# Ternary feed-forward: row transposes by DMA instead of by TensorE, and two roundings moved to ScalarE

## The reference, cut to what matters

```
def _quant_weight(w):                      # ternary
    scale = jnp.mean(jnp.abs(w)) + EPS
    return jnp.clip(jnp.round(w / scale), -1.0, 1.0) * scale
def _quant_act(x):                         # 8 bits, one scale for each row
    scale = jnp.maximum(jnp.max(jnp.abs(x), axis=-1, keepdims=True), EPS) / 127.0
    return jnp.clip(jnp.round(x / scale), -128.0, 127.0) * scale
def bitlinear(x, w): return einsum('bsi,oi->bso', _quant_act(x), _quant_weight(w))

gate = sigmoid(bitlinear(layernorm(x), w_gate))     # 512 -> 2048
up   = bitlinear(layernorm(x), w_up)                # 512 -> 2048
x    = x + tanh(g_ffn[0]) * bitlinear(gate * up, w_down)    # 2048 -> 512
```

## Time and profile before

| | us |
|---|---|
| median of 3 runs | 1298.64 (1296.31 to 1298.73) |
| the profiled execution | 1298.14 |
| its span, first to last instruction | 1296.4 |
| the feed-forward, 573 to 789 us of the span | about 216 |

### The profile page before, as it was taken

How to read it: one execution, slowest core, us unless ns; L and a number is a source line. 1 busy time by engine, 2 the same in 40 slices (tenths; PEclk the granted TensorE clock), 3 DMA queues, 4 the chain that set the end, 5 groups by cost and what they waited for, 6 DMA issues and landing times. The chain is left out here.

```text
span 1296.4 us, 14519 instructions
## 1 busy us (share of the span) xinstructions
PE 1108.1 (85%) x4802; PEld 449.3 (35%) x4802; DVE 1020.2 (79%) x1560; ACT 668.9 (52%) x783; POOL 526.6 (41%) x403
## 2 busy tenths in 40 slices
PE   4976399999999999838999994999999998189686
PEld 2543022222222222103444442444444444034232
DVE  5678498888888888218999982888888877777888
ACT  1645048787887887925566563110000000686896
POOL 5757010534534534530011012878887884000021
PEclk9989569999999999969999997999999998599879
DMA  9799633545445544132111101121221220000011
GB/s 321 244 317 339 197 107 118 158 125 169 139 126 170 139 125 153 53 126 83 49 49 32 49 17 36 49 60 55 65 65 49 65 65 16 0 1 1 0 66 65
DMA packets 65215, 131.74 MB, mean 102 GB/s; under 512 B 13864, under 2 KB 31656, under 8 KB 61552
## 3 DMA queue, kind: packets, MB, share of 16 engines
q1 hardware_dynamic: 65152, 130.95, 31.6%
HBM read 106.53 MB, written 22.02 MB: 99 GB/s over the span
## 5 line engine op out<-in xcount | busy, mean ns | idle before, releaser
L804 DVE TENSOR_REDUCE mneg<-ps_m 128x1 f32<-128x512 f32 x512 | 319.6, 681 | 53.0 <-PE ps_m L717 52.6
L1345 PE MATMUL ps_y<-kv,toeplitz_sb 128*128 128x512 f32 x640 | 279.4, 595 | 8.9 <-POOL kv L1257 8.9
L685 ACT ACTIVATE probs<-ps_s 128x1024 f32<-128x1024 f32 x256 | 250.9, 1022 | 51.8 <-PE ps_s L739 51.7
L717 PE MATMUL ps_m<-k_stack,q_stack 112*128 112x512 bf16 x512 | 186.6, 405 | 17.1 <-DMA k_stack<-mask_k 16.0
L1345 PEld LDWEIGHTS ps_y<-kv,toeplitz_sb 128*128 128x128 f32 x640 | 121.0, 191 | 155.2 <-issue 155.2
L739 PE MATMUL ps_s<-q_stack,k_stack 112*128 112x512 bf16 x512 | 153.3, 383 | 10.7 <-ACT probs L685 10.5
L749 PE MATMUL ps_o<-probs,v_all 128*17 128x512 f32 x1024 | 134.7, 598 | 0.4 <-ACT probs L685 0.4
L1257 POOL TENSOR_TENSOR kv<-vT,ctxT_sb 128x2048 f32<-128x2048 f32 x32 | 118.8, 3712 | 39.1 <-PE ps_y L1345 32.3
L980 PE MATMUL ps_g<-w,xT_f 128*128 128x512 bf16 x512 | 120.0, 383 | 7.1 <-DVE h_f L1127 6.3
L1411 DVE TENSOR_TENSOR z<-ps_y,ctxT_sb 128x1024 f32<-128x1024 f32 x64 | 77.9, 1217 | 47.1 <-PE ps_y L1345 47.1
L1310 ACT ACTIVATE w_anchor<-w_f 128x512 f32<-128x512 f32 x32 | 20.1, 628 | 180.6 <-DMA w_f<-in_w 180.6
(11 more groups left out here) (159 smaller groups left out, 1628.3 us busy)
## 6 DMA issues: line engine op xcount, KB each, us to landing
w_sweep<-in_w SPq DMA_DIRECT2D x8, 1536.0 KB, 10.2
q_stack<-q_parts SPq DMA_DIRECT2D x96, 128.0 KB, 4.1
k_stack<-k_parts SPq DMA_DIRECT2D x96, 128.0 KB, 3.9
w_sweep<-in_w SPq DMA_DIRECT2D x16, 768.0 KB, 5.5
w_sweep<-in_w SPq DMA_DIRECT2D x16, 512.0 KB, 3.5
toeplitz_sb<-in_toeplitz SPq DMA_DIRECT2D x32, 256.0 KB, 2.7
w_f<-in_w SPq DMA_DIRECT2D x32, 256.0 KB, 2.9
k_parts<-qk_part SPq DMA_DIRECT2D x24, 256.0 KB, 7.0
```

The costliest lines, as they stand in the source:

```text
L685: nc.scalar.activation(pr[:, k % 2, 2 * slot:2 * slot + 2, :], S[:, 2 * slot:2 * slot + 2, :], ACT.Exp).then_inc(exp_done, 1)
L717: nc.tensor.matmul(M[:, bank(j), :], Q[0:ROWS, slot, hd, tc * P:(tc + 1) * P], K[0:ROWS, slot, hd, :], start=True, stop=True).then_inc(max ...
L804: nc.vector.tensor_reduce(mneg[:, h, tile % LT, tile // LT:tile // LT + 1], M[:, bank(j), :], AX.X, ALU.max, negate=True).then_inc(max_red, 1)
L1345: mm = nc.tensor.matmul(Y[:, q % 3, l2, :], T[:, g % 2, (lt - m) * P:(lt - m + 1) * P], kv[:, g % 2, m, :], start=(m == 0), stop=(m == lt))
```

## The change

- Both transposes are DMAs on SP's queue: xT from xq and hT from hq, each one instruction (L932, L939). TensorE's transposes, the PSUM tiles XTP and HTP and ScalarE's copies `copy_x` and `copy_h` are gone.
- ScalarE centres the rows (`centre(t+2)`, behind the sigmoid of chunk 3) and rounds them (`round_x(t+1)`, two instructions, behind the sigmoid of chunk 1). VectorE's `prepare` keeps the maximum and the scales.
- `round_h(t-1)` moves from behind the sigmoid of chunk 1 to behind that of chunk 2, `take_down(t-2)` from behind that of chunk 2 to behind that of chunk 3 and `centre`.
- The maxima of h are two of 1024 columns (`half_max`) in place of four of 512. The maximum of the weight piece moves from chunk 2 to chunk 1.
- The four loads of ctxT (1 MB each) are issued in tile 0 behind the transposes of x, no longer ahead of everything.
- The loop over pairs of tiles is written out.

```diff
-    tile(0, 0, True, False)
-    tile(1, 1, False, False)
-    with eng.Fori(1, n // 2 - 1) as i:
-        tile(2 * i, 0, False, False)
-        tile(2 * i + 1, 1, False, False)
-    tile(n - 2, 0, False, False)
-    tile(n - 1, 1, False, True)
+    for t in range(n):
+        tile(t, t % 2, t == 0, t == n - 1)
...
+                def turn_x(t, par):
+                    sp.wait_ge(xq_ready, t + 1)
+                    if t >= 2:
+                        sp.wait_ge(gu_done, NCH * (t - 1))
+                    sp.dma_start(xT[:, par], xq[:, par, :], transpose=True).then_inc(xT_ready[par], 16)
+                def turn_h(t, par):
+                    sp.wait_ge(hq_ready, t + 1)
+                    if t >= 2:
+                        sp.wait_ge(down_done, t - 1)
+                    sp.dma_start(hT[:, par], hq[:, par, :], transpose=True).then_inc(hT_ready[par], 16)
...
+                    if not last:
+                        turn_x(t + 1, 1 - par)
+                    if not first:
+                        turn_h(t - 1, 1 - par)
+                    if first:
+                        for lt in range(LT):
+                            sp.dma_start(core.cT[:, lt], A["ctxT"][lt * P:(lt + 1) * P]).then_inc(core.cT_loaded, 16)
+                    if last:
+                        turn_h(t, par)
+                turn_x(0, 0)
                 over_tiles(sp, ROWT, tile)
...
-                def turn_x(t, par):
-                    pe.wait_ge(xq_ready, t + 1)
-                    for lt in range(LT):
-                        mm = nc.tensor.transpose(XTP[:, lt * P:(lt + 1) * P], xq[:, par, lt * P:(lt + 1) * P],
-                                                 core.ident16[:])
-                    mm.then_inc(xt_done, 1)
...
                         pe.wait_ge(d_taken, t)
-                    for half in range(2):
-                        pe.wait_ge(hT_ready, 2 * t + half + 1)
-                        for k in range(half * KT // 2, (half + 1) * KT // 2):
-                            mm = nc.tensor.matmul(D[:], hT[:, par, k, :], wd[:, k, :], start=(k == 0),
-                                                  stop=(k == KT - 1))
+                    pe.wait_ge(hT_ready[par], 16 * (t // 2 + 1))
+                    for k in range(KT):
+                        mm = nc.tensor.matmul(D[:], hT[:, par, k, :], wd[:, k, :], start=(k == 0), stop=(k == KT - 1))
                     mm.then_inc(down_done, 1)
...
-                        if c == 2 and not last:
-                            turn_x(t + 1, 1 - par)
-                        if c == 3 and not first:
-                            turn_h(t - 1, 1 - par, same(t, 1))
...
+                def centre(t, par):
+                    nc.scalar.activation(xn[:, par, :], X[:, t, :], ACT.Identity, bias=nb[:, t:t + 1],
+                                         scale=core.rstd[:, t:t + 1]).then_inc(xn_ready, 1)
+                def round_x(t, par):
+                    act.wait_ge(rx_ready, t + 1)
+                    nc.scalar.activation(xn[:, par, :], xn[:, par, :], ACT.Identity, bias=core.magic,
+                                         scale=sc[:, par, RX:RX + 1]).then_inc(xr_ready, 1)
+                    act.wait_ge(xr_ready, t + 1)
+                    if t >= 2:
+                        act.wait_ge(xT_ready[par], 16 * (t // 2))
+                    nc.scalar.activation(xq[:, par, :], xn[:, par, :], ACT.Copy, bias=-MAGIC).then_inc(xq_ready, 1)
+                centre(0, 0)
+                centre(1, 1)
+                round_x(0, 0)
...
-                        if c == 1 and not first:
+                        if c == 1 and not last:
+                            round_x(t + 1, 1 - par)
+                        if c == 2 and not first:
                             round_h(t - 1, 1 - par)
-                        if c == 2 and not last:
-                            copy_x(t + 1, 1 - par, first)
-                        if c == 2 and not early(t):
+                        if c == 3 and t + 2 < ROWT:
+                            centre(t + 2, par)
+                        if c == 3 and not early(t):
                             take_down(t - 2, par, same(t, 2))
-                        if c == 3 and not first:
-                            copy_h(t - 1, 1 - par)
...
-                    step(nc.vector.tensor_scalar(xn[:, par:par + 1, :], X[:, bass.ds(t, 1), :],
-                                                 core.mean[:, bass.ds(t, 1)], core.rstd[:, bass.ds(t, 1)],
-                                                 ALU.subtract, ALU.mult))
+                        dve.wait_ge(x_step, 2 * n + steps[0])
+
+                    dve.wait_ge(xn_ready, t + 1)
                     step(nc.vector.tensor_reduce(col(par, AMAX), xn[:, par, :], AX.X, ALU.max,
                                                  apply_absolute_value=True))
                     step(nc.vector.tensor_scalar(col(par, SX), col(par, AMAX), QEPS, 1.0 / 127.0, ALU.max, ALU.mult))
-                    step(nc.vector.reciprocal(col(par, RX), col(par, SX)))
-                    step(nc.vector.tensor_scalar(xn[:, par, :], xn[:, par, :], col(par, RX), MAGIC, ALU.mult, ALU.add))
-                    step(nc.vector.tensor_scalar(sc[:, par, GS:US + 1], core.w_scale[:, 0:2], col(par, SX), None,
-                                                 ALU.mult))
-                    nc.vector.tensor_scalar(xq[:, par, :], xn[:, par, :], -MAGIC, None, ALU.add)\
-                        .then_inc(xq_ready, 1)
+                    nc.vector.reciprocal(col(par, RX), col(par, SX)).then_inc(rx_ready, 1)
+                    nc.vector.tensor_scalar(sc[:, par, GS:US + 1], core.w_scale[:, 0:2], col(par, SX), None, ALU.mult)\
+                        .then_inc(scales_ready, 1)
...
-                    dve.wait_ge(hmax_ready, NCH * (t + 1))
-                    step(nc.vector.tensor_reduce(col(par, HM), sc[:, par, H0:H0 + NCH], AX.X, ALU.max))
+                    dve.wait_ge(hmax_ready, 2 * (t + 1))
+                    step(nc.vector.tensor_tensor(col(par, HM), col(par, H0), col(par, H0 + 1), ALU.max))
+                    dve.wait_ge(scales_ready, t + 1)
...
-                def chunk_max(t, par, c):
-                    dve.wait_ge(h_ready, NCH * t + c + 1)
-                    nc.vector.tensor_reduce(col(par, H0 + c), h[:, par, c * L:(c + 1) * L], AX.X, ALU.max,
+                def half_max(t, par, i):
+                    dve.wait_ge(h_ready, NCH * t + 2 * i + 2)
+                    nc.vector.tensor_reduce(col(par, H0 + i), h[:, par, 2 * i * L:2 * (i + 1) * L], AX.X, ALU.max,
                                             apply_absolute_value=True).then_inc(hmax_ready, 1)
...
-                        if c:
-                            chunk_max(t, par, c - 1)
+                        if c == 2:
+                            half_max(t, par, 0)
                         if c == 0 and not last:
-                            if not first:
-                                dve.wait_ge(xt_done, t)
                             prepare(t + 1, 1 - par, t + 1)
-                        if c == 2:
-
+                        if c == 1:```

ScalarE, a tile in the middle of the layer, before. sg_f is the sigmoid, hq_f the rounded inner row, xT_f and hT_f the turned rows.

```order
L1035 ACTIVATE sg_f<-ps_g,sc_f 128x512 [waits h_ready,gu_done]
L1016 ACTIVATE hq_f<-h_f 128x2048 [waits ht_done,ha_ready]
L1035 ACTIVATE sg_f<-ps_g,sc_f 128x512 [waits h_ready,gu_done]
L1002 ACTIVATE xT_f<-ps_xt 128x512 [waits xt_done]
L1023 ACTIVATE down_sums<-ps_d,sc_f 128x512 [waits xf_updated,down_done]
L1035 ACTIVATE sg_f<-ps_g,sc_f 128x512 [waits h_ready,gu_done]
L1008 ACTIVATE hT_f<-ps_ht 128x1024 [waits ht_done] x2
```

More of the change, by code:

```diff
@@ L935, in tile @@
                         .then_inc(w8c_loaded[par], 16)
-                for lt in range(LT):
-                    sp.dma_start(core.cT[:, lt], A["ctxT"][lt * P:(lt + 1) * P]).then_inc(core.cT_loaded, 16)
+                    if not last:
[8 more added lines that the diff above has]
+                turn_x(0, 0)
                 over_tiles(sp, ROWT, tile)
@@ L942, in _ @@
             def _(pe):
-                def turn_x(t, par):
-                    pe.wait_ge(xq_ready, t + 1)
-                    for lt in range(LT):
-                        mm = nc.tensor.transpose(XTP[:, lt * P:(lt + 1) * P], xq[:, par, lt * P:(lt + 1) * P],
-                                                 core.ident16[:])
-                    mm.then_inc(xt_done, 1)
-                def turn_h(t, par, first):
-                    pe.wait_ge(hq_ready, t + 1)
-                    for half in range(2):
-                        if not first:
-                            pe.wait_ge(hT_ready, 2 * t + half - 1)
-                        for k in range(KT // 2):
-                            c = half * (KT // 2) + k
-                            mm = nc.tensor.transpose(HTP[:, half, k * P:(k + 1) * P], hq[:, par, c * P:(c + 1) * P],
-                                                     core.ident16[:])
```

(42 more changed lines are left out.)

27 lines of the change are left out of this document (11 added, 16 removed).

## The result

The changed kernel takes 1324.57 us (median of 4, 1321.57 to 1325.41) against 1298.39 (1296.31 to 1298.73): ratio 1.0201, 95% interval 1.0182 to 1.022, or 26.2 us more. 1333 was forecast, in a range of 1308 to 1445.

A forecast was written before the change was run, and what follows sets the result against it. VectorE was taken to set the pace, then chain two at 13.8 us a tile. Start +2.0, tiles 0 to 3 +2.7, eleven tiles +18.7 and last tile +11.2 gave +34.6 on 1298.1: 1333 us, range 1308 to 1445.

The forecast's parts named there:

- What bounds the kernel: Mid feed-forward: VectorE sets the pace at 12.06 us a tile, PE 1.7 us behind with a need of 10.35.
- what the change takes away: VectorE loses 1.46 us of outer-row work and 0.1 on maxima, falling to 10.5 us a tile; PE to 10.35.
- Chain one: Per-tile loop through ScalarE's rounding and late down-sum scaling, GpSimd and VectorE's statistics: 12.5 to 12.7 us a tile.
- The price of d: Time of h's DMA transpose from issue to semaphore: 5.8 us, from 2,048 small packets at 0.030 us each.
- chain two: Per-tile loop from h's rounding through its DMA transpose, down matmuls and chunk 2: 8.0 us plus d.
- fast DMA: Rival: d under 4.7 us, so chain one decides; +14.7 us, 1313 us; chance 0.22.
- The transpose of x: DMA of x in each tile: 2.9 us, with some 6 us of cover, costing nothing but at the start.
- Tiles 0 to 3: First feed-forward tiles: +2.7 us, an estimate; ctxT loads stand behind the first transposes, VectorE's weight piece behind them.
- Last tile: End of the feed-forward, where nothing covers the DMA transposes of h: PE's waits add +11.2 us together.
- The clock: PE's idle 2.8 us a tile might lower its clock, costing 22 us; left out of the sum, kept in the range.

The follow-up runs named there:

- e6: Kernel e4 with both transposes back on TensorE and PSUM, with ScalarE's copies: 1289.17 us, ratio 0.9935 to the kernel before the change.
- e1: Changed kernel with ScalarE's scaling of the down sum ahead of the centring, both behind chunk 3's sigmoid: 1316.74 us, ratio 1.0153 to before.
- e2: Changed kernel with the scaling of the down sum back behind chunk 2's sigmoid, ahead of the rounding of h: 1315.89 us, ratio 1.0155 to before.
- e5: Changed kernel with each DMA transpose of h done twice, first into an unread scratch tile, PE waiting for both: 1340.85 us, ratio 1.0341 to before.
- e3: Changed kernel with the four ctxT loads issued one each in tiles 4, 6, 8 and 10: 1316.46 us, ratio 1.0161 to before.
- e4: Changed kernel with e3's loads, h then x rounded behind chunk 1, down sum behind chunk 2: 1286.02 us, ratio 0.9922 to before.

## Why the prediction held, and which step of it failed

- **What bounds the kernel; what the change takes away.** Right that both engines were nearly full, that both were relieved, and that neither is full now. Wrong that PE stood 1.7 us behind VectorE: the 10.35 leaves out its 20 transposes, of which those of `h` alone are 1.06 a tile, and the earlier trace rows has PE busier than VectorE (23.55 against 23.10). With the transposes on PE and VectorE relieved the tile was 11.47 (e6), 0.6 under the old one.
- **Chain one.** Right but for one kind of link: 12.5 to 12.7 forecast, 13.05 measured. (The second figure should be 12.8: 2.97 less 2.68 is 0.29, where the forecast adds 0.2.) Statistics' wait 1.9 forecast, 1.94 measured; its exact place is confirmed by e1 (the centring's link is worth itself, 0.70) and e2 (the chain gone, the wait gone). The link mis-sized is ScalarE's 128x512 with scale and bias from columns, taken from the plain ones of the earlier trace rows at 0.63. The group lines of the changed kernel (mean ns after the busy time):

```profile
L1000 ACT ACTIVATE xn_f<-xn_f,columns,sc_f 128x512 f32<-128x512 f32 x16 | 13.0, 813 | 62.2 <-DVE sc_f L1067 62.2
L994 ACT ACTIVATE xn_f<-X,x_shift_f,rstd 128x512 f32<-128x512 f32 x16 | 12.8, 806 | 0.5 <-DVE x_shift_f L1102 0.5
...
L1005 ACT ACTIVATE xq_f<-xn_f 128x512 bf16<-128x512 f32 x16 | 10.1, 630 | 0.5
```

  Two of them are in the loop: centring to sum 0.70 where 0.52 was forecast, first to second instruction of `round_x` 0.84 where it was 0.67, and 0.06 less at the sigmoid behind them: the 0.3 that are missing. The Trainium skill has the difference ("ScalarE: Activation LUTs", What ACT_TABLE_LOAD costs): each scale or bias taken from a column adds about 93 ns to an ACTIVATE, and the trace agrees with 0.18 for two.
- **The price of d.** This is the step that failed: 5.8 taken, 3.7 measured, so that chain two (11.7) stays under chain one and the mechanism is the rival's, *fast DMA*. The packets were counted right and priced wrong: 0.030 us each was read off 432 packets of another stage; the transposes' take 0.019. With that price the same formula gives 1.9 + 2,048 x 0.019 / 16 = 4.3, below the 4.7 that separates the two cases; the 0.6 from there to 3.7 stay open. I had both ends of the range and chose between them by the kind of packet; the nearer row by size was the ordinary load of 512 KB, 3.5. The Trainium skill's rule ("Advanced Engine Details and Errata", X-Bar Transpose), that a transposing DMA is as fast as an ordinary one, agrees with this trace in the time to landing: 3.7 beside 3.8 for an ordinary load of the same 512 KB. In queue time the transpose is dearer, 2,048 x 0.019 = 39 us beside 256 x 0.096 = 25. The 1309 ns for a block in the Trainium skill ("VectorE: DVE Perf Modes", The three transpose paths) cannot be added up: sixteen blocks took 3.7, 0.23 each.
- **Chain two itself** is right where it decides: e2 (12.3 by it, 12.25 measured) and e5 (13.7, 13.67).
- **The transpose of x** lands in 2.3 (2.9 forecast), but the "6 us of cover" are wrong: `round_x` waits for `prepare`, behind the product, and PE stands 1.18 us a tile for it. By the loop read above it cost nothing, since the pace was set elsewhere; no run tests this by itself.
- **Tiles 0 to 3.** +2.7 forecast, +8.25 measured. I named the cause (the weight piece is behind the `ctxT` loads) and gave it an estimate with no row under it, though one was there: 4 MB with 8.2 us to land, ahead of a piece for which VectorE's whole order waits. e3 takes 8.6 away by moving the loads. The miss hid part of the other: e3, without it, is at 1316.46, near the fast rival's 1313.
- **Last tile.** +11.2 forecast, +5.4 measured: d smaller by 2.0 at two places, and no 2.8 ahead of `down(13)`, is 6.9 less; the clock behind the idle stretches (4.92 for 3.61, 6.10 for 5.30) puts 2.1 back; the remaining 1.0 I did not take apart.
- **The clock.** Left out of the sum, rightly: 1.00 in the middle with PE idle for 1.2, and also in e5 with 2.55. By the times of the matmuls it did fall after 8.19, 4.59 and 6.34 us of idleness, in the first tiles and in the last, which the forecast left out in both.

So the range and the sign were right, and 1333 was 8.4 off, by two errors of opposite sign: the tiles and the tail 13 too much, the first tiles 5.6 too little. That it came so near is luck: the fast rival, whose mechanism was the right one, said 1313 and was 11.6 off, since it too had put the first tiles at little (+1.7). The time alone would have spoken for the wrong chain. The chances were worse than the number: the mechanism that decided had 0.22, the one that did not 0.52. Still open are the loop of e4 and why its tiles vary.

## What to carry to other kernels

Taking work off the busiest engine buys nothing if the instructions go onto a loop: follow one value from an engine and back to itself a tile later, and put ScalarE's results in the order in which somebody waits for them. The same instructions were 2% slower in one order and 0.8% faster in another (0.4% of the difference is the place of the big loads on SP). A DMA transpose is cheap in the middle of a pipeline and dear at its ends, where its 3.8 us and the slower matmuls behind the wait stand alone; and it makes an engine's queue of loads into a queue with waits, so that big loads nobody needs yet must go behind.
